# Loading the next stage's first tiles one stage ahead, and awaiting last stores later, in a two-layer decoder on one core

## The reference, cut to what matters

```python
x = x + L0_attn(layernorm(x))                 # causal, 16 heads of 16, rotary positions
x = x + L0_xattn(layernorm(x), ctx, ctx)      # queries from x, 77 keys and values from ctx, masked
x = x + L0_ffn(layernorm(x))                  # 8 experts, the best one for each row
x = x + L1_attn(layernorm(x))                 # 16 heads of 64
x = x + L1_xattn(layernorm(x), ctx, ctx)
h = x + attention(rmsnorm(x, ln1_w))          # 16 heads of 16, not causal
return h + moe(rmsnorm(h, ln2_w))             # 8 experts, the best two for each row
```

## Time and profile before

| | us |
|---|---|
| median of 3 runs | 2794.97 (2788.21 to 2799.53) |
| the profiled execution | 2786.01 |
| its span, first to last instruction | 2784.2 |
| outside the span | 1.8 |

### The profile page before, as it was taken

How to read it: one execution, slowest core, us unless ns; L and a number is a source line. 1 busy time by engine, 2 the same in 40 slices (tenths; PEclk the granted TensorE clock), 3 DMA queues, 4 the chain that set the end, 5 groups by cost and what they waited for, 6 DMA issues and landing times. The chain is left out here.

```text
span 2784.2 us, 44955 instructions
## 1 busy us (share of the span) xinstructions
PE 2383.0 (86%) x16140; PEld 1265.0 (45%) x16140; DVE 1613.4 (58%) x2656; ACT 1134.9 (41%) x2059; POOL 1022.7 (37%) x798
## 2 busy tenths in 40 slices
PE   6589997876987995999999998867859999958998
PEld 5433335335986771333333332732612222246887
DVE  5778874655433335666666663246769999653222
ACT  3436665331112331444444443233426777811221
POOL 3511002411441113677777776121440000015665
PEclk9869999556998997999999999965869999978999
DMA  5432212427995553222222221442341121046665
GB/s 151 115 71 63 70 33 80 107 76 211 345 338 162 193 193 109 68 82 88 80 70 83 85 84 40 144 102 62 111 122 38 40 55 36 6 112 175 201 186 150
DMA packets 233718, 315.80 MB, mean 113 GB/s; under 512 B 57289, under 2 KB 174307, under 8 KB 233030
## 3 DMA queue, kind: packets, MB, share of 16 engines
q1 hardware_dynamic: 192228, 241.72, 27.9%
q0 software_dynamic: 35232, 66.39, 9.7%
q10 hardware_dynamic: 6082, 5.35, 1.1%
HBM read 215.86 MB, written 96.84 MB: 112 GB/s over the span
## 5 line engine op out<-in xcount | busy, mean ns | idle before, releaser
L1636 ACT ACTIVATE a_probs<-a_cols 128x512 f32<-128x512 f32 (+3 forms) x896 | 445.2, 549 | 245.6 <-PE a_cols L1566 163.4
L1658 DVE TENSOR_REDUCE a_mxw<-a_rows 128x2 f32<-128x1024 f32 (+1 forms) x448 | 475.5, 1099 | 69.5 <-PE a_rows L1524 42.2
L2085 DVE TENSOR_REDUCE a_mxw<-a_rows 128x2 f32<-128x1024 f32 x256 | 313.4, 1224 | 208.0 <-PE a_rows L1923 206.2
L2063 ACT ACTIVATE a_probs<-a_cols 128x1024 f32<-128x1024 f32 x256 | 261.9, 1025 | 266.4 <-PE a_cols L1952 247.7
L1904 POOL TENSOR_TENSOR a_sums<-a_sums,a_probs 128x1024 f32<-128x1024 f32 x128 | 309.8, 2420 | 99.3 <-ACT a_probs L2063 86.6
L1566 PE MATMUL a_cols<-a_qs,a_ks 50*128 50x512 bf16 (+7 forms) x1792 | 279.0, 368 | 14.2 <-DMA a_qs<-a_nparts 8.1
L1948 PE MATMUL a_cols<-a_qf,a_kf 64*128 64x512 f32 x1024 | 266.6, 599 | 0.0
L2381 PE MATMUL e_psU<-e_xT,e_w 128*128 128x128 f32 (+1 forms) x1472 | 254.0, 332 | 11.9 <-issue 8.5
L1594 PE MATMUL a_out<-a_probs,a_vs 128*17 128x256 f32 (+4 forms) x3328 | 258.6, 384 | 0.2 <-ACT a_probs L1636 0.2
L1524 PE MATMUL a_rows<-a_ks,a_qs 48*128 48x512 bf16 (+3 forms) x896 | 176.4, 390 | 86.4 <-DVE a_mxw L1658 39.5
L1966 PE MATMUL a_out<-a_probs,a_vs 128*64 128x512 f32 x1024 | 247.8, 605 | 0.0
(11 more groups left out here) (282 smaller groups left out, 3404.7 us busy)
## 6 DMA issues: line engine op xcount, KB each, us to landing
e_w<-in_w SPq DMA_DIRECT2D x46, 1024.0 KB
e_w<-in_w SPq DMA_DIRECT2D x69, 512.0 KB
a_qs<-q_scratch SPq DMA_DIRECT2D x336, 64.0 KB, 2.2
qk_wide_scratch<-t_f SPq DMA_DIRECT2D x32, 512.0 KB
q_scratch<-t_parts POOLq DMA_DIRECT2D x56, 192.0 KB
a_ks<-k_scratch SPq DMA_DIRECT2D x144, 64.0 KB, 2.5
vw_scratch<-t_v SPq DMA_DIRECT2D x8, 1040.0 KB
a_vs<-vw_scratch SPq DMA_DIRECT2D x16, 520.0 KB
```

What stands on the lines that cost most here:

```text
L1636: act.activation(pr[ug % RING][:, 2 * hp + e, c0:512], psC[(2 * at + e) % 3][:, 0:512 - c0], ACT.Exp, scale=scale).then_inc(ex_done, 1)
L1658: dve.tensor_reduce(mxw[w][:, a, hp, :, t % 4:t % 4 + 1], src[:, :, 0:n], AX.X, ALU.max).then_inc(s_free, 1)
L2063: act.activation(pr[i][:], psC[i % 2][:], ACT.Exp, scale=scale).then_inc(ex_done, 1)
L2085: dve.tensor_reduce(mxw[:, j % 2, :, j // 2:j // 2 + 1], psR[:], AX.X, ALU.max).then_inc(s_free, 1)
```

## The change

- New global tiles hold what crosses a stage's end: `first_q`, `first_k`, `first_v` (group 0 of the next attention), `first_rows` (chunks 0 and 1 of the next token stage, and all later chunks of it), and the tiles from which the last stores are made (`last_parts`, `last_values`, `last_on`). Their semaphores are global too.
- A token stage ahead of an attention issues group 0's loads on SP: the main ones behind the row load of chunk 6, after waiting for the stores of chunks 0 to 3; the rest behind the row load of chunk 7.
- An attention issues the next token stage's two first row loads on SP ahead of its own last stores (in the wide one: ahead of the last sums' way through memory).
- SP no longer waits for the last stores at the end of t0, a0, t1, a1, t4, a4, t5 and a5. Who reads them waits: group 1's loads and those of every odd group, and chunk 4's row load. The wide attention keeps its wait.
- In a cross attention SP issues group 2's loads ahead of `place(0)`, not behind it, and the products of zeros fall from 20 to 1, those between slots to none.
- The twelve mask copies of a0 move into the context stage's VectorE list, and two blocks of ones into its POOL list.

```diff
@@ token_stage
-                        wait(sp, y_ready, c - 1)
-                        sp.dma_start(ot[p][:], attn[:, c * C:(c + 1) * C].rearrange("(k p) t -> p k t", p=P)
-                                     ).then_inc(o_ld[p], 16)
+                        if c >= 2:
+                            wait(sp, y_ready, c - 1)
+                            if c == NC // 2 and attn_from is not None:
+                                sp.wait_ge(*attn_from)
+                            sp.dma_start(ot[p], attn[:, c * C:(c + 1) * C].rearrange("(k p) t -> p k t", p=P)
+                                         ).then_inc(o_ld[p], 16)
+                    if front and next_group is not None:
+                        if front[0] == NC - 2:
+                            if next_group.ones:
+                                sp.wait_ge(ones_set, 2)
+                            for p in range(2):
+                                sp.wait_ge(f_out[p], NC // 4 * store_per_use)
+                                if v_cols:
+                                    sp.wait_ge(v_out[p], NC // 4 * 16)
+                            next_group.load_main(sp)
+                        if front[0] == NC - 1:
+                            next_group.load_rest(sp)
...
                     store_last(sp, 0)
-                    sp.wait_ge(last_out, n_last)
@@ context_stage, VectorE
+                for name, src in (("ident", "identb"), ("maskS", "maskS"), ("maskT", "maskT")):
+                    for half in range(2):
+                        for e in range(2):
+                            dve.tensor_copy(G["halves"][name][half][64 * e:64 * (e + 1), :], G[src][64 * half:64 * (half + 1), :])
@@ cross_attention_stage
-                fetch(0)
+                fetch(2)
                 place(0)
-                fetch(2)
                 prefetch.load(sp)
...
+                sp.wait_ge(stored[(NG - 2) % 3], ((NG - 2) // 3 + 1) * H * 16)
+                rows_ahead.load(sp)
                 sp.wait_ge(o_done, 2 * NG)
                 for dst, src in list(stores_of(NG - 1))[:2]:
                     sp.dma_start(dst, src).then_inc(last_stored, 16)
-                sp.wait_ge(last_stored, 16 * H)
...
-                zero_products(pe, G, psO[:], 20)
+                zero_products(pe, G, psO[:], 1)
...
+                act.wait_ge(*scores_from)
                 load(act, 1, 0)
@@ narrow_attention_stage
-                load_main(sp, 0, 0)
-                load_rest(sp, 0, 0)
                 place(0, 0)
...
-                sp.wait_ge(last_stored, 16 * H)
@@ wide_attention_stage, SP, the last group
                         store(u - 1, 0, p, r)
+                        for w in range(2):
+                            sp.wait_ge(stored[w], 16 * (n_groups - 1))
+                        rows_ahead.load(sp)
                         sums_to_rows(u, 1)
```

More of the change, by code:

```diff
@@ L92, in wait, with __init__, scores, load_main @@
         eng.wait_ge(sem, value)
+MAIN_PARTS = ((0, 0), (0, 1), (1, 0))
+REST_PARTS = ((2, 0), (0, 2), (1, 1))
+CROSS_MAIN = ((0, 1), (0, 0), (1, 0))
+CROSS_REST = ((0, 2), (1, 1), (2, 0))
+class FirstGroup:
+    def __init__(self, G, tag, q, k=None, v=None, ones=False):
+        self.G, self.q, self.k, self.v, self.ones = G, q, k, v, ones
+        self.main_loaded, self.rest_loaded = G["first_main_loaded"][tag], G["first_rest_loaded"][tag]
+        self.n_main = 16 * 6 * (1 + (k is not None))
+        self.n_rest = self.n_main + 16 * (v is not None)
+    def scores(self, eng, x, tile, which, kind, sem):
+        narrow = self.k is not None
+        parts = ((MAIN_PARTS, REST_PARTS) if narrow else (CROSS_MAIN, CROSS_REST))[kind]
+        for s, pair in enumerate(parts):
+            for e in range(2):
+                eng.dma_start(tile[64 * e + 16 * s:64 * e + 16 * s + 16, kind].rearrange("r m a t -> r (m a t)"),
+                              x[pair[which], 0, 32 * e:32 * (e + 1)].rearrange("(r m) t -> r (m t)", m=2)).then_inc(sem, 16)
+    def load_main(self, eng):
+        self.scores(eng, self.q, self.G["first_q"], 0, 0, self.main_loaded)
+        if self.k is not None:
+            self.scores(eng, self.k, self.G["first_k"], 1, 0, self.main_loaded)
+    def load_rest(self, eng):
+        self.scores(eng, self.q, self.G["first_q"], 0, 1, self.rest_loaded)
+        if self.k is not None:
+            self.scores(eng, self.k, self.G["first_k"], 1, 1, self.rest_loaded)
+        if self.v is not None:
+            eng.dma_start(self.G["first_v"][:].rearrange("p (a t) h x -> p a (t h x)", a=2),
+                          self.v.rearrange("g o p t x -> (g o) p (t x)")[0:2].rearrange("a p x -> p a x")
+                          ).then_inc(self.rest_loaded, 16)
+class FirstRows:
+    def __init__(self, G, tag, attn):
+        self.G, self.attn, self.kf, self.loaded = G, attn, attn.shape[0] // P, G["attn_loaded"][tag]
+    def load(self, eng):
+        for c in range(2):
+            eng.dma_start(self.G["first_rows"][c][:, 0:self.kf, :], self.attn[:, c * C:(c + 1) * C].rearrange("(k p) t -> p k t", p=P)
+                          ).then_inc(self.loaded[c], 16)
 def zero_products(pe, G, bank, n):
@@ L324, in token_stage @@
         if attn is not None:
-            ot = [st.sb(f"attnT{p}", [P, kf, C]) for p in range(2)]
+            ot = [G["first_rows"][p][:, 0:kf, :] for p in range(2)]
         wo, wfs, bfs, fsc = weights.wo, weights.wf, weights.bf, weights.fscale
@@ L522, in step @@
                         store_values(pool, middle)
+                if next_group is not None and next_group.ones:
+                    for e in range(2):
+                        pool.memset(G["first_q"][64 * e + 32:64 * e + 64, 0], 1.0).then_inc(ones_set, 1)
+                    pool.wait_ge(ones_set, 2)
                 in_stages(step)
@@ L897, in _ @@
                         pool.memset(G["ctx_keys"][l][64 * e + 32:64 * e + 64, 0], 1.0)
+                for e in range(2):
+                    pool.memset(G["first_k"][64 * e + 32:64 * e + 64, 0], 1.0)
             @block.sync
@@ L1019, in cross_attention_stage @@
     with Stage(nc, tag) as st:
-        qs = [st.sb(f"qs{p}", [P, 2, 2, 2, 512], BF16) for p in range(4)]
+        qs = [G["first_q"]] + [st.sb(f"qs{p}", [P, 2, 2, 2, 512], BF16) for p in (1, 2, 3)]
         pr = [st.sb(f"probs{r}", [SC, H, 512]) for r in range(RING)]
@@ L1372, in narrow_attention_stage @@
         if causal:
-            mask = {n: [st.sb(f"{n}{b}", [P, P], BF16) for b in range(2)] for n in ("ident", "maskS", "maskT")}
-            masks_set = st.sem("masks_set")
+            mask = G["halves"]
         main_ld = [st.sem(f"main_loaded{p}") for p in range(4)]
@@ L1620, in _ @@
             def _(act):
-                first = list(scores_loads(0, 0, 1))
-                for n, (dst, src) in enumerate(first):
-                    if n == 4:
-                        act.wait_ge(ones_set[0], 2)
-                    act.dma_start(dst, src).then_inc(main_ld[0], 16)
-                load_rest(act, 0, 1)
                 for g in range(NG):
@@ L1731, in _, with wide_attention_stage @@
                 divide(NG - 1, 1)
-def wide_attention_stage(nc, G, tag, *, q, k, qb, kb, v, o, sums, bias, prefetch):
+def wide_attention_stage(nc, G, tag, *, q, k, qb, kb, v, o, sums, bias, prefetch, rows_ahead):
     hd = 64
@@ L1746, in wide_attention_stage @@
     with Stage(nc, tag) as st:
-        qs = [st.sb(f"qs{p}", [P, S], BF16) for p in range(2)]
-        ks = [st.sb(f"ks{p}", [P, S], BF16) for p in range(2)]
+        rows_home = G["first_q"][:].rearrange("p k m w t -> p (k m w t)")
+        qs = [rows_home[:, S * p:S * (p + 1)] for p in (0, 1)]
+        ks = [rows_home[:, S * p:S * (p + 1)] for p in (2, 3)]
         qf = [st.sb(f"qf{p}", [P, S]) for p in range(2)]
@@ L2617, in weights, with around, rows_from @@
             return TokenWeights(nc, G, tag, **what)
+        narrow = dict(q=Q16, k=K16, v=V16)
+        firsts = {"a0": FirstGroup(G, "a0", **narrow), "a1": FirstGroup(G, "a1", Q16, ones=True), "a4": FirstGroup(G, "a4", Q16),
+                  "a5": FirstGroup(G, "a5", **narrow)}
+        rows_of = {tag: FirstRows(G, tag, attn) for tag, attn in (("t1", OA), ("t2", OA), ("t4", OW), ("t5", OA), ("t6", OA))}
+        def around(tag, ahead, behind, n_last):
+            return dict(first=firsts[tag], rows_ahead=rows_of[behind], scores_from=(G["last_stored"][ahead], 16 * n_last))
+        def rows_from(tag):
+            return (G["last_stored"][tag], 16 * 4)
         ctx = [context_loads(G, 0, CK[0], CM), context_loads(G, 1, CK[1], None)]
```

121 lines of the change are left out of this document (65 added, 56 removed).

## The result

| kernel | median us | runs | ratio to before, 95% interval | profiled execution us | span us |
|---|---|---|---|---|---|
| before | 2794.06 | 6 | | 2786.01 | 2784.2 |
| changed | 2781.59 | 6 | 0.9955 (0.994 to 0.9969) | 2774.06 | 2772.3 |

A forecast was written before the change was run, and what follows sets the result against it. Token stages were held bound by TensorE, an all-engine chain at their ends and landings at their starts, only landings attacked. 55.2 us won less 31.7 and 3 lost gave 20.5, so 2774.5 from the 2795.0 median; range 2752 to 2792.

The forecast's parts named there:

- Hand-overs into token stages: Attention to token stage, four times: TensorE starts after the bare barrier of 0.83 us, rows already there; 20.9 us won.
- Into narrow attentions: Token stage to a0 and a5: VectorE's first maximum comes earlier, by 13.4 and 9.6 us; 23.0 us won.
- Into cross attentions: Token stage to a1 and a4: first columns earlier, limited by group 1's loads and `place(0)`; 5.1 and 5.7, 10.8 us won.
- a3: Wide attention to t4: row wait of 5.7 us saved, small store of last sums 5.2 us later behind 2 MB; 0.5 won.
- Chunk 7: t1, t4, t5: TensorE stalls 8.8, 6.0, 11.4 us for late rows; with low clock, less time won back, 31.7 us lost.
- The low clock: Behind the stalls at chunk 7: TensorE's clock falls, costing 2.5 us each in t1 and t5, 1.5 in t4; 6.5 together.
- The 1.0 us to be won back: Behind the stalls in t1, t4, t5: some 1 us regained where ScalarE and VectorE had been short ahead of it.
- Context stage: Twelve mask copies on VectorE, about one per POOL fill, delay the first addition on the path to t0; 3 us lost.
- (a): Rival: chunk 7's rows in t1, t4, t5 are not late, gain whole at 52 us, so 2743; chance 0.13.
- (b): Rival: clock stays low to stage end behind the three stalls, 43 us lost for 6.5, so 2811; chance 0.07.
- (c): Rival: shorter hand-over idle keeps the clock up; t1, t6 start at full speed, 2 to 3 us each, 2767; chance 0.10.
- (d): Rival: SP's waits for chunks 0 to 3 make group 0's loads late for the attentions; about 2785, chance 0.02.

The follow-up runs named there:

- waits-only kernel: Changed kernel with only the waits for stores of chunks 0 to 3 before chunk 7's row load, group 0's loads all behind it; 2767.3 us, ratio 0.9896.
- the rows first: Changed kernel with chunk 7's row load in t1, t4, t5 issued before the four store waits and group 0's main loads; 2743.99 us, ratio 0.981.
- the end waits: Kernel with the rows first, but SP again waits for the last stores at the end of eight stages; 2761.41 us, ratio 0.9869.

## Why the prediction was right in its course and 8 us off in its sum

**Hand-overs into token stages** (20.9 forecast, 19.6 measured). The mechanism is as forecast; the bare barrier is 1.0 us here (426.28 to 427.30 at t1), not 0.83, and the last tenths go to the first product behind it.

**Into narrow attentions** (23.0, measured 21.5). a0 gives 13.2 of 13.4. a5 gives 8.3 of 9.6: this stage begins 2.7 us behind the end of the last issue, not 0.83 (a0 1.6). SP waits 2.0 us of the 2.7 for another engine. POOL, which must wait for its stores of chunk 6 (issued until 2033.98), is the likely one, but no run settles it.

**Into cross attentions** (10.8, measured 10.7). The sum is right. In a1 less came at the first columns than forecast (3.1 for 5.1), because `place(0)` came 0.65 us later than forecast and the placed rows then took 2.6 us to land behind the twelve loads; 1.35 came later. The products of zeros were counted at nothing, and the kernel that puts them back doesn't contradict this.

**a3** (0.5 won, 1.3 lost). The wait for the last sums was given as growing from 1.7 to about 7 us; it is 7.7. The rows hide 5.2 us at t4, not 5.7. The step that failed is a size: the 2 MB keep the engines busy for 8.1 us, not 7.7 (from 1715.34 to about 1723.5), and the store is seen to land 0.8 us behind their end, not with it.

**Chunk 7** (31.7 lost, 37.2 measured) holds two thirds of the error. The stalls were given as 8.8, 6.0 and 11.4 and are 10.5, 6.4 and 14.0. The step that was mis-sized is the landing of the rows: 3.0 us were taken from the start of t1, where nothing stands ahead of them, and it is 4.0 in t1 and 5.1 in t5, behind six and twelve loads on the same queue; with t4's 5.9 for 5.5 this is 3.5 of the 4.6 us by which the stalls were given too short. The waits-only kernel shows how much of it is the loads ahead: its landings are 3.5 and 3.2 us in t1 and t5, so nearly 2 us of it in t5, and in t1 half of the 1.0. The waits for chunk 3's stores took 0.4 us longer than forecast in t1 and t5 (SP goes on 3.4 us after TensorE has asked for chunk 7). The low clock cost about what was said: 8 products at the restart take 3.58 and 3.77 us for 1.89, in t4 32 take 9.44 for 7.07, some 6 us for the 6.5. In t4 the stall was held to be at the edge of what lets the clock fall; the granted clock was 0.50 in the two us behind its 6.4, and in the waits-only kernel it came down to 0.50 (1800 to 1802) even behind 3.8. The 1.0 us to be won back behind the stalls did not appear.

**Context stage** (3, measured 2.7 at t0's start, 2.9 at t0's end). One copy got through per fill, as read from a0's rows: VectorE's first six copies start and end with POOL's six fills, the other six take 0.19 us each.

**The rivals.** (a) was wrong as a forecast, but its time was right for the kernel that it describes: 2743 were given for a change whose rows aren't late, and with the rows first 2744.0 were measured. That the two agree so closely is in part luck: the stretches of that kernel's profile add up to 46.2 us won, and (a) had 52. So 38 us of a possible 51 were lost by four waits and six or twelve loads that stand ahead of one row load. (b) The clock did not stay low. Three windows of the changed kernel, with columns us, then busy us of PE, PEld, DVE, ACT, POOL, PEclk, DMA share, GB/s, behind the stalls of t1, t4 and t5:

```profile
469.00:482.00 13.00, 6.14 (x30) 4.65 (x29) 4.93 (x12) 7.85 (x18) 5.45 (x6) 0.99 0.18 61
...
1810.00:1825.00 15.00, 11.05 (x53) 9.00 (x51) 3.96 (x10) 7.16 (x17) 5.41 (x6) 1.00 0.11 34
...
2012.00:2036.00 24.00, 16.84 (x77) 13.20 (x75) 12.74 (x30) 13.16 (x35) 11.76 (x12) 0.98 0.31 101
```

Within 4 to 5 us the full clock is back, as after the idle of before. (c) did not happen in general: t1's first 16 products take 5.26 us for 6.37, but t6's 6.18 for 5.27. (d) The loads were in time everywhere.

The median is a term of its own. The gap of 9 us between the profiled execution of before and the median was carried over, and it held: 7.5 for the changed kernel. This is luck, since it depends on which execution is profiled: with the rows first the profile lies 2.2 us above the median, with the end waits 8.3 above. All of the miss is in the sum of the stages.

## What to carry to other kernels

Loads for the next stage are worth what the hand-over shows, some 4 to 13 us each here, but they must be issued behind everything on their queue that the present stage still waits for: twelve small issues and four waits ahead of one row load cost 15 us in one stage. Before a load is moved ahead of a small store or read, look at what goes to the same DMA engines in the next 8 us, since another queue gave back 2 us of 6 only, and look for an earlier place; a3's rows could be had 18 us sooner, in a stretch with slack. With the next stage's loads at hand, a wait that is dropped at a stage's end gave 1.4 to 2.9 us, eight times, with nothing hidden.

## What the runs showed of the hardware that I had not expected

- A landing gets slower by many small loads ahead of it on its queue: 256 KB of rows took 3.2 us from issue to use in t5 with none ahead, 5.1 and 5.4 behind twelve loads of 64 KB. Behind six it was 4.0 and 3.8 for 3.5 in t1, and no difference in t4.
- An 8 KB store beside 2 MB on a different queue still took 5.5 us (7.7 on the same, 1.7 alone), though it landed before the 2 MB were through.
- ScalarE's copies of 64 x 128 bf16 took 0.31 us each beside POOL's fills, where VectorE's took as long as the fill, 1.1 or 1.8.
- Shorter idle ahead of a stage did not spare the low clock at its start: t2's, t5's and t6's first 16 products took 6.27, 6.00 and 6.18 us after some 4.5 us of idle.
